# A four-layer graph network on one core: the engines' hand-over in the dense stage, the source rows of the first edge layer, and the mask's type

## The reference, cut to what matters

```python
# layer 0
edge_input = concat(h[src], edge_attr_32)
messages = gelu(edge_input @ mW1 + mb1) @ mW2 + mb2
gates = sigmoid(gelu(edge_input @ gW1 + gb1) @ gW2 + gb2)
aggregated = segment_sum(messages * gates, dst)
update = gelu(concat(h, aggregated) @ uW1 + ub1) @ uW2 + ub2
x = x + layernorm(h + update) * ln_g + ln_b
# layer 1
e = (relu(concat(h[src], h[dst]) @ Wm1 + bm1) @ Wm2 + bm2) * edge_attr_96
x = x + relu(concat(h, segment_sum(e, dst)) @ Wu1 + bu1) @ Wu2 + bu2
# layer 2: segment_sum(h[src] @ W + b, dst) / max(deg, 1)
# layer 3: three graph convolutions, norm_src and norm_dst around segment_sum
```

## Time and profile before

| what | us |
|---|---|
| median of 3 runs (6865.93 to 6893.16) | 6881.36 |
| the profiled execution's own time | 6877.96 |
| its span, first to last instruction | 6876.1 |
| PE busy, share of the span | 4438.8, 65% |
| DVE busy | 3951.5, 57% |
| ACT busy | 3522.4, 51% |
| POOL busy | 4259.0, 62% |

### The profile page before, as it was taken

How to read it: one execution, slowest core, us unless ns; L and a number is a source line. 1 busy time by engine, 2 the same in 40 slices (tenths; PEclk the granted TensorE clock), 3 DMA queues, 4 the chain that set the end, 5 groups by cost and what they waited for, 6 DMA issues and landing times. The chain is left out here.

```text
span 6876.1 us, 104878 instructions
## 1 busy us (share of the span) xinstructions
PE 4438.8 (65%) x19614; PEld 2908.5 (42%) x19614; DVE 3951.5 (57%) x12722; ACT 3522.4 (51%) x8822; POOL 4259.0 (62%) x4323
## 2 busy tenths in 40 slices
PE   5768888888886777776887776554555555322222
PEld 2225566555663333333444443444444444222222
DVE  5667777777775666665555554666666344322222
ACT  6987887888885776775555553222222222111110
POOL 0005454555546777775777776775775776677777
PEclk9998988999887888887888887555555555555555
DMA  0003333333332333332444444665554899433332
GB/s 16 0 5 85 102 102 97 102 102 102 102 98 73 77 78 75 76 75 68 118 119 116 119 118 103 161 160 141 123 129 120 119 126 127 79 76 78 79 84 66
DMA packets 958039, 652.70 MB, mean 95 GB/s; under 512 B 730453, under 2 KB 834785, under 8 KB 957946
## 3 DMA queue, kind: packets, MB, share of 16 engines
q1 hardware_dynamic: 819962, 483.05, 25.0%
q0 software_dynamic: 137984, 168.67, 16.2%
HBM read 420.24 MB, written 232.62 MB: 95 GB/s over the span
## 5 line engine op out<-in xcount | busy, mean ns | idle before, releaser
L610 POOL DMA_INDIRECT got<-info_d,idx x784 | 776.8, 991 | 1258.6 <-issue 732.5
L610 POOL DMA_INDIRECT xs<-t,idx x1176 | 1110.8, 945 | 502.4 <-issue 347.7
L1031 PE MATMUL bank<-w,aggT 96*128 96x96 f32 (+1 forms) x3136 | 773.9, 428 | 470.5 <-DVE aggT L1293 470.4
L1024 PE MATMUL bank<-ident,msg 128*96 128x128 f32 (+1 forms) x1568 | 424.3, 426 | 991.3 <-ACT msg L848 819.7
L1031 PEld LDWEIGHTS bank<-w,aggT 96*128 96x128 f32 (+1 forms) x3136 | 703.5, 329 | 581.8 <-issue 500.7
L610 POOL DMA_INDIRECT xs<-c,idx x784 | 748.3, 954 | 314.9 <-issue 233.1
L848 ACT ACTIVATE msg<-xs,now 128x96 f32<-128x96 f32 x784 | 229.3, 363 | 1297.3 <-DMA xs<-c,idx 679.3
L1024 PEld LDWEIGHTS bank<-ident,msg 128*96 128x96 f32 (+1 forms) x1568 | 290.1, 218 | 1052.0 <-ACT msg L848 678.8
L1293 DVE TENSOR_TENSOR_SCAN aggT<-goes,aggT,bank 96x512 f32<-96x512 f32 (+1 forms) x490 | 621.2, 1268 | 135.0 <-DMA goes<-goes_d 63.1
L701 ACT ACTIVATE hd<-xd,nmr,rstd 128x96 f32<-128x96 f32 x1568 | 599.1, 454 | 27.0 <-DVE nmr L1182 27.0
L610 POOL DMA_INDIRECT xs<-in_x_dram,idx x392 | 473.3, 1207 | 173.9 <-issue 119.2
(11 more groups left out here) (189 smaller groups left out, 10722.2 us busy)
## 6 DMA issues: line engine op xcount, KB each, us to landing
goes<-goes_d SPq DMA_DIRECT2D x392, 256.0 KB
t<-xo SPq DMA_DIRECT2D x392, 192.0 KB, 3.5
t<-xn SPq DMA_DIRECT2D x294, 192.0 KB, 2.3
xd<-in_x_dram SPq DMA_DIRECT2D x196, 192.0 KB, 2.4
out_dram<-oo SPq DMA_DIRECT2D x196, 192.0 KB
goes<-goes_d SPq DMA_DIRECT2D x196, 192.0 KB
xd<-t SPq DMA_DIRECT2D x196, 192.0 KB, 4.0
c<-xn SPq DMA_DIRECT2D x196, 192.0 KB, 3.7
```

What stands on the lines that cost most here:

```text
L610: nc.gpsimd.indirect_dma_start(out=into, out_offset=None, in_=table, in_offset=bass.IndirectOffsetOnAxis(ap=indices, axis=0)).then_inc(don ...
L1024: ins = nc.tensor.transpose(bank[g.at(2)][0:m, c * P:(c + 1) * P], msg[:, g.at(2), c, 0:m], ident[:])
L1031: ins = nc.tensor.matmul(tok(bank[2 + g.at(2)], m)[:, c, :], aggT[0:m, g.at(3), c * P:(c + 1) * P], w2[:] if k == 0 else w3[:, k - 1, :], ...
```

## The change

Four edits. (1) In the dense stage the functions of PE and ACT get lags that are one larger from `evac1` and `evac2` on (`evac1` 0 to 1, `z1` 0 to 1, `gelu1` 1 to 2, `out1` 1 to 2, and likewise for layer 1's; `norm_y` 2 to 3), and the order within a step changes on ACT, PE and DVE. The lags of `plus_x` and `finish_x` stay. (2) In the dense stage POOL also gathers x[src], two indirect DMAs of 128 rows a round into `xs`, and SP stores them to a new DRAM table `x_src` in the order of the edges (`x_src_store`, lag 5, ahead of `info_keep`). (3) In e0 POOL gathers only x[dst]; SP loads the source rows from `x_src` (`xs_load`, one plain DMA a round). (4) The mask `goes` and its DRAM copy are float16; a start-up scratch buffer that lay in it moves to `hd`.

```diff
@@ -130,8 +130,9 @@
         dstp = dram("dstp", (E_PAD + 2,), I32)
-        goes_d = dram("goes_d", (E_PAD,))
+        goes_d = dram("goes_d", (E_PAD,), F16)
         info_d = dram("info_d", (HI * LO, 2))
+        x_src = dram("x_src", (E_PAD, D))
         t1 = dram("t1", (E_PAD + N, D))
@@ -165,7 +166,7 @@
         st_p = sb("st_p", [P, ET], I32)
-        st_goes = sb("st_goes", [P, ET])
+        st_goes = sb("st_goes", [P, ET], F16)
         edge_pad = sb("edge_pad", [1, 2], I32)
@@ -214,8 +215,7 @@
         msg = sb("msg", [P, 2, G, D + 1])
-        goes = sb("goes", [P, 3, GE])
-        iota_lo_i = goes[:, 0:2, :].rearrange("p s e -> p (s e)")[:, 0:LO].bitcast(I32)
+        goes = sb("goes", [P, 3, GE], F16)
         tanh_g = sb("tanh_g", [D, 2, GE])
@@ -228,6 +228,7 @@
         degi, cum = (xn[0:HI, :, :, :].rearrange("p s c d -> p (s c d)")[:, i * LO:(i + 1) * LO] for i in range(2))
+        iota_lo_i = hd[:].rearrange("p s c d -> p (s c d)")[:, 1024:1024 + LO].bitcast(I32)
         has, home = (b[0:HI, :, :, :].rearrange("p s c d -> p (s c d)")[:, 0:LO] for b in (xo, oo))
@@ -298,13 +299,13 @@
                    dict(x_in=(6, 1, 1), x1_out=(6, 1, 1), x2_out=(3, 1, 1), o_out=(3, 1, 1), idx_in=(2, 1, GT),
-                        got=(2, 2 * GI * GT, GT), kept=(2, 1, GT)))
+                        got=(2, 2 * GI * GT, GT), kept=(2, 1, GT), xs=(6, GI, 1), c_out=(6, 1, 1)))
         dn["root"] = Count(sem("root_dn"))
...
                             tok_g=1, tok=1, gate=1, msg=1, agg=1, z=1, g=1, u=1, y=1, my=1, norm_y=1, yx=1, xb=1, xr=1),
-                   edge_slots)
+                   {name: edge_slots[name] for name in edge_slots if name != "xs"} | dict(x_in=(6, 1, 1)))
         more("attr", (EG - 1) % 3, 16)
@@ -421,6 +422,10 @@
                     sp.sem_inc(sp_turn, 1)
+                    for i in range(GT):
+                        was = g.shift(i)
+                        need(sp, dn["xs"][was.at(6)], freed(was, 6, GI))
+                        sp.sem_inc(sp_turn, 1)
                     idx_columns(dn, g, NG, GI, slice(0, 2))
@@ -458,15 +463,22 @@
-            pipelined(sp, NG, [(info_idx, 0), (dense_load, 1), (info_keep, 6), (dense_store_x1, 8), (dense_store_x2, 11)])
+            def x_src_store(g):
+                need(sp, dn["xs"][g.at(6)], landed(g, 6, GI))
+                sp.sem_inc(sp_turn, 1)
+                sp.dma_start(x_src[bass.ds(g.j * GI * P, GI * P), :].rearrange("(c p) d -> p c d", p=P),
+                             xs[:, g.at(6), 0:GI, :]).then_inc(dn["c_out"][g.at(6)].sem, 16)
+
+            pipelined(sp, NG, [(info_idx, 0), (dense_load, 1), (x_src_store, 5), (info_keep, 6), (dense_store_x1, 8), (dense_store_x2, 11)])
...
                             was = g.shift(i)
-                            need(sp, ph["xs"][was.at(6)], freed(was, 6, G))
-                            sp.sem_inc(sp_turn, 1)
+                            if "xs" in ph:
+                                need(sp, ph["xs"][was.at(6)], freed(was, 6, G))
+                                sp.sem_inc(sp_turn, 1)
                             if "xd" in ph:
@@ -509,10 +521,17 @@
-                pipelined(sp, EG, [(gather_idx(ph, planes), 0), (edge_load, 3), (goes_load, 5), (edge_store, done)])
+                def xs_load(g):
+                    need(sp, ph["norm_s"], g.j - 5)
+                    sp.sem_inc(sp_turn, 1)
+                    sp.dma_start(xs[:, g.at(6), :, :], edge_view(x_src, g.j * GE)).then_inc(ph["x_in"][g.at(6)].sem, 16)
+
+                pipelined(sp, EG, [(gather_idx(ph, planes), 0)] + ([(xs_load, 1)] if ph is e0 else []) + [(edge_load, 3), (goes_load, 5), (edge_store, done)])
             sp.wait_ge(goes_out, 16)
-            edge_phase(e0, t1, slice(0, 2), 11)
+            for s in range(6):
+                need(sp, dn["c_out"][s], ended(NG, 6, s))
+            edge_phase(e0, t1, slice(1, 2), 11)
             for s in range(3):
@@ -625,6 +644,10 @@
                                dn["got"][half(g)])
+                need(pool, dn["c_out"][g.at(6)], freed(g, 6))
+                pool.sem_inc(pool_turn, 1)
+                for c in range(GI):
+                    gather(xs[:, g.at(6), c, :], a["x"][:, :], idx[:, half(g), 0, col + c:col + c + 1], dn["xs"][g.at(6)])
@@ -645,10 +668,11 @@
                     pool.sem_inc(pool_turn, 1)
+                    for c in range(G if ph is e1 else 0):
+                        gather(xs[:, g.at(6), c, :], t[:, :], idx[:, half(g), 0, col + c:col + c + 1], ph["xs"][g.at(6)])
+                    which = 1 if ph is e1 else 0
                     for c in range(G):
-                        gather(xs[:, g.at(6), c, :], t[:, :], idx[:, half(g), 0, col + c:col + c + 1], ph["xs"][g.at(6)])
-                    for c in range(G):
-                        gather(xd[:, g.at(6), c, :], t[:, :], idx[:, half(g), 1, col + c:col + c + 1], ph["xd"][g.at(6)])
+                        gather(xd[:, g.at(6), c, :], t[:, :], idx[:, half(g), which, col + c:col + c + 1], ph["xd"][g.at(6)])
@@ -738,7 +762,7 @@
             def norm_y(g):
-                standard(dn, g, tok(bank[2 + 4 * g.at(2)]), 2, 1)
+                standard(dn, g, tok(bank[2 + 4 * g.at(2)]), 3, 1)
@@ -764,7 +788,7 @@
             act.wait_ge(weights_in, 16 * n_weights[0])
-            pipelined(act, NG, [(gelu1, 1), (relu2, 5), (norm1, 0), (norm2, 4), (norm_y, 2), (evac1, 0), (evac2, 4)])
+            pipelined(act, NG, [(evac1, 1), (evac2, 5), (gelu1, 2), (relu2, 6), (norm_y, 3), (norm1, 0), (norm2, 4)])
@@ -933,7 +957,7 @@
             pe.wait_ge(idx_step, 1)
-            pipelined(pe, NG, [(out1, 1), (out2, 5), (tr1, 0), (tr2, 4), (z1, 0), (z2, 4)])
+            pipelined(pe, NG, [(z1, 1), (z2, 5), (out1, 2), (out2, 6), (tr1, 0), (tr2, 4)])
@@ -1217,7 +1241,7 @@
                 dve.sem_inc(dve_turn, 1)
-                pair_stats(tok(bank[2 + 4 * g.at(2)]), mv[:, g.shift(2).at(3), 1, :, :]).then_inc(dn["my"].sem, 1)
+                pair_stats(tok(bank[2 + 4 * g.at(2)]), mv[:, g.shift(3).at(3), 1, :, :]).then_inc(dn["my"].sem, 1)
@@ -1259,12 +1283,12 @@
             def dense_state(g):
-                return upto(g, NG, (dn["norm"], g.j - 2), (dn["norm_y"], g.j - 4), (dn["norm2"], g.j - 6),
-                            (dn["mx"], g.j + 1), (dn["my"], g.j - 1), (dn["mz"], g.j - 3))
+                return upto(g, NG, (dn["norm"], g.j - 2), (dn["norm_y"], g.j - 5), (dn["norm2"], g.j - 6),
+                            (dn["mx"], g.j + 1), (dn["my"], g.j - 2), (dn["mz"], g.j - 3))
             dve.wait_ge(info_out, 16)
-            pipelined(dve, NG, [(times_g(dn), 4), (finish_x, 7), (plus_x, 4), (finish_o, 7), (plus_b, 4), (mom_x, 0),
-                                (mom_y, 2), (mom_z, 4), (roots_of(dn, dense_state), 0, NG + 4)])
+            pipelined(dve, NG, [(finish_x, 7), (mom_y, 3), (finish_o, 7), (mom_x, 0), (times_g(dn), 4), (plus_x, 4),
+                                (plus_b, 4), (mom_z, 4), (roots_of(dn, dense_state), 0, NG + 4)])
             for s in range(3):
@@ -1299,7 +1323,10 @@
                 def edge_moments(g):
-                    need(dve, ph["xs"][g.at(6)], landed(g, 6, G))
+                    if first:
+                        need(dve, ph["x_in"][g.at(6)], landed(g, 6))
+                    else:
+                        need(dve, ph["xs"][g.at(6)], landed(g, 6, G))
                     need(dve, ph["xd"][g.at(6)], landed(g, 6, G))
```

## The result

| | us |
|---|---|
| predicted | 6628 (6535 to 6765) |
| after, median of 4 runs | 7260.53 (7255.95 to 7270.57) |
| before, median of 4 runs on the same chip | 6881.18 (6865.93 to 6893.16) |
| ratio, 95% interval | 1.0555 (1.0531 to 1.0578) |

A forecast was written before the change was run, and what follows sets the result against it. It took POOL's gathers to bound the first edge stage and the other engines' hand-over the dense stage, where POOL would take over. Gains of 31, 207 and 15 us made 253 off 6877.96: 6628 as median, range 6535 to 6765.

The forecast's parts named there:

- Dense stage, the hand-over: Dense stage: with the new lags a loop through PE and ACT takes 7.13 us a round, 0.3 under 7.44.
- the loss to the clock: Dense stage: 0.42 us a round of today's loss carried over, so PE, ACT and DVE could do 7.55 us.
- POOL's 7.80: Dense stage: with six gathers a round POOL becomes the bound at 7.80 us a round, ends 7.50 and 8.18.
- The draining behind it: End of the dense stage: POOL ends at 2045 us and e0 starts at 2063, 31 us earlier than before.
- The new waits and the extra DMA on SP: Dense stage: the new waits on POOL and SP and one more plain DMA a round on SP cost nothing.
- e0: First edge stage: without the x[src] gathers the round falls from 11.21 to 9.1 us, gain 207 us, ends 275 and 109.
- The mask: Conv k = 2: 16-bit mask halves its bytes, scan time unchanged, gain 15 us from a range of 0 to 47.
- The lock: Dense stage: DVE's two-SBUF-input work blocks POOL, 9.70 us a round, 372 us more, 7000 in all; chance 0.04.
- e0's exchange taking the gap: First edge stage: PE's and ACT's waits grow, round 10.1 us, gain 109 instead of 207, total 6726; chance 0.17.
- That x_src brings nothing: First edge stage: bound by DVE's chain of roots at 11.2 us, only 46 us left, total 6835; chance 0.03.
- The one with the sign right: Dense stage: the slower rival, POOL blocked by DVE's two-SBUF-input work, 7000 us in all; chance 0.04.
- the same sum: Whole kernel: gains of 31, 207 and 15 us, 253 off 6877.96, giving 6625, or 6628 for the median.

The follow-up runs named there:

- dve_order: The changed kernel with DVE's dense step reordered, finish_x and finish_o at lag 8 and the moments last before the roots: 6953.97 us, ratio 1.0110.
- nogap: dve_order with out1, out2 first on PE, and on ACT gelu1, relu2 ahead of the evacuations and norm_y ahead of norm1: 6555.03 us, ratio 0.9511.
- finish8: The changed kernel with only the lag of finish_x and finish_o raised from 7 to 8: 7209.96 us, ratio 1.0462.
- full_order: nogap with DVE's dense step reordered, finish_x behind mom_x instead of after times_g: 6530.57 us, ratio 0.9477.
- act_order: dve_order with gelu1 and relu2 ahead of the evacuations on ACT and norm_y last: 7113.03 us, ratio 1.0341.
- lags_only: The kernel before with only edit (1), the dense stage's new lags and orders on PE, ACT and DVE: 7589.33 us, ratio 1.1034.
- gather_only: The changed kernel with edit (1) undone, edits 2 to 4 kept: 6550.23 us, ratio 0.9519.

## Why the dense stage lost its clock

How the low clock and the gap hang together is read from one stretch at 0.50 each of before, after, dve_order and nogap, in this order (columns as in the earlier trace rows):

```profile
1444.40:1454.40 10.00, 10.00 (x36) 7.42 (x35) 5.57 (x20) 6.29 (x16) 3.78 (x4) 0.50 0.28 81
```

```profile
938.00:1010.00 72.00, 63.83 (x220) 47.29 (x220) 35.26 (x128) 39.92 (x98) 34.85 (x36) 0.50 0.29 83
```

```profile
1058.00:1208.00 150.00, 133.85 (x466) 100.28 (x465) 78.70 (x287) 82.07 (x205) 82.27 (x84) 0.50 0.31 89
```

```profile
1280.30:1290.40 10.10, 10.09 (x36) 7.65 (x36) 7.70 (x32) 7.28 (x18) 7.76 (x8) 0.50 0.70 215
```

In before, a round at low clock is 36 matmuls in 10.0 us, and PE does not wait at all: its own instructions have grown longer and cover ACT's. It is granted the full clock again after 10.2 us, in each of the 33 such stretches of that dense stage (mean clock 0.87; the stage's start and end, where PE has little to do, are left out here and below). In after, 220 matmuls are 6.1 rounds: 11.8 us each, PE busy 10.4 of them and waiting 1.35 for gelu1. This wait is 1.35 us at either clock, since evac2 and gelu1 start when PE has finished and PE starts when they have. Here 38 of the 40 low stretches last 24 to 120 us (in dve_order they last 14 to 150, in finish8 68 to 140 but for three of 3.4), and at full clock the round is 7.59 us, at low clock 11.8 (13.3 where the clock changes within it). The mean of 11.52 is mostly the time at low clock. nogap has the 10.0 us back, in most of its low rounds without a wait, and its full clock comes back after 10.2 us in 61 of 63 stretches, after 6.8 in the other two.

The full clock is also lost sooner in after. It holds for 10.2 us at a time, in 40 of 41 stretches; in before for 7 to 96 us, 35 on average. One such stretch of after as a window, and two of its rows of PE:

```profile
1009.70:1019.90 10.20, 5.68 (x36) 4.07 (x35) 8.58 (x29) 6.33 (x17) 3.46 (x3) 1.00 0.31 89
```

```profile
1011.25 1.07 PE L912 MATMUL bank<-hdT,uw 96*96 96x512 f32 x2 [1.35 <-ACT u L775]
...
1018.21 0.65 PE L919 MATMUL bank<-ident,hd 128*96 128x128 f32 x4 [2.38 <-ACT hd L725]
```

PE is busy for 5.7 of these 10.2 us: beside the 1.35 for gelu1 it waits 2.38 us for norm1 (`hd`), which on ACT stands behind norm_y, and norm_y waited 3.66 us for the roots there. In the full-clock stretches of before PE is busy for 75 to 81%.

Two things speak against the length of a wait as the whole cause. In 18 of nogap's 61 stretches of 10.2 us PE did stand still, for up to 0.61 us, and the clock came back all the same; in full_order it did so after waits of up to 0.79 us. And in act_order the clock stayed low through stretches in which no wait of PE was longer than 0.49 us, eight of its 27, of 65 to 120 us. The longest:

```profile
690.60:810.10 119.50, 115.35 (x396) 85.65 (x396) 64.92 (x243) 69.82 (x177) 64.41 (x67) 0.50 0.32 92
```

What is shown: edit (1)'s orders and lags make the loss (lags_only, gather_only); the low round of 11.8 us is PE's 10.4 and the wait of 1.35, with the ring closed or open (after, finish8); the time is lost in long stretches at 1.2 instead of 2.4 GHz; and two moves of order, with the lags kept, bring the stage back (nogap). Every order with the wait of 1.35 us in each round has low stretches of 120 us and more. That this wait is what keeps the clock low is argued and not shown: act_order stays low without it, and nogap changes ACT's and PE's order at once, so that which of the two the clock answers to was not separated. What the chip counts was not measured, and is not guessed.

## Why the prediction was wrong, by its own steps

**The step that failed** is in "Dense stage, the hand-over": "With today's loss to the clock (7.86 - 7.44 = 0.42) PE, ACT and DVE could do a round in 7.55 us." The loop itself was found, but a round wholly at full clock took 7.59 us and not 7.13, more than the 7.33 of before: the ring below held it (with the ring open, in finish8, three such rounds took 6.9 to 7.4). The larger part is the clock. The same loop holds all of PE's step and a stretch in which PE must stand still. At half the clock PE's part of it is 10.4 us and the standing still is added, 11.8; and the loss to the clock, taken over as 0.42, was the price in a kernel whose PE had no such gap. The loss became 11.52 - 7.59 = 3.9 us a round. The numbers for it stood in the text: the earlier trace rows showed the clock at 0.77 beside 1.00, and nothing was asked about what ends a low stretch.

**A ring not seen**: out2 to finish_x, roots, norms, tr2 and back in two rounds. By itself it costs little (finish8, 50 us), though with DVE's whole order turned 318 us came back (dve_order), which stays unexplained beyond the 50.

**POOL's 7.80** was right where nothing hid it: 7.80 in full_order, 7.99 in gather_only, 7.97 in nogap. The draining behind it was taken too short: in full_order POOL's last gather started at 2045 us, as forecast, but e0 at 2078 and not 2063. So even this version gains 15 us before e0 where 31 were forecast, and gather_only loses 25. In after POOL was not the bound. The new waits and the extra DMA on SP cost nothing that can be seen: gather_only and full_order have them all.

**e0** was right in mechanism and too small in size. ACT's wait for the roots, 189.5 us, is no longer among the waits; one single wait of 20.7 us for roots is left, on another line, at the start of the stage. The other terms were held too high: 9.1 us a round forecast, 8.00 measured; gain 318 instead of 207, outside its ends (109 to 275). The two waits for hid, 0.48 and 0.34 us, and 0.5 for tr were added to ACT's 7.88. Measured, those for hid come to 0.5 and 1.5 us over the whole stage, the wait for tr to 24.8 (0.27 a round), and ACT's own work is 755 / 98 = 7.70; 7.70 + 0.27 = 7.97 is the round. PE's work for the same matmuls fell from 8.75 to 7.31 us a round, with the clock at 0.98 instead of 0.85. PE was seen as kept "busier" and granted "more clock"; the drop of 1.44 us that this makes was not carried through.

**The mask** was right, 15 us forecast and 15 measured; that the figure is met so exactly is luck, since 15 was picked from a range of 0 to 47. Its scan and the DMA of k = 2 (5715 to 6240 us, packets, MB, share), after:

```profile
L1317 DVE TENSOR_TENSOR_SCAN aggT<-goes,aggT,bank 96x512 f32<-96x512 f16 x392 | 497.2, 1268 | 111.1 <-DMA goes<-goes_d 47.2 <-PE bank L1015 29.7 <-PE bank L1048 25.4
...
L1317 DVE TENSOR_TENSOR_SCAN aggT<-goes,aggT,msgT 96x512 f32<-96x512 f16 x98 | 124.9, 1274 | 0.5 <-DVE msgT L1340 0.5
```

```profile
q1 hardware_dynamic: 81688, 33.22, 24.3%
...
goes<-goes_d SPq DMA_DIRECT2D x100, 128.0 KB, 5.5
```

1.268 and 1.274 us with a 16-bit operand against 1.269 and 1.274: the width changes nothing in DVE's time here. The queue holds 24.3% instead of 32.1, with 33.22 MB instead of 46.04, and DVE's wait for the mask in that stage fell from 63.1 to 47.2 us.

**The rivals.** The lock did not come (mean gathers of 0.94 to 1.00 us in the dense stage of every kernel). The e0 row that spoke for it is weaker than it was read: that gather had started 0.25 us before the first of the DVE operations, and these ran on for 0.55, 1.27 and 0.53 us, no longer than elsewhere, so only POOL was held up. e0's exchange taking the gap (0.17) did not either: the opposite. That x_src brings nothing (0.03): no. The slower case that came was not among them. The one with the sign right was priced on POOL's side, while edit (1), the only one that touches PE, was given a gain with no way to lose. With that edit left out the same sum would have had 6550 in its range, though partly by luck: e0's extra gain of more than 110 us covers the 56 us by which the dense stage fell short (25 lost where 31 were to be gained).

## What to carry to other kernels

When engines pass work to and fro, look for a stretch in which the matrix engine waits for something that starts only when it stops; price this loop once for each clock level seen in the trace, since another engine's work that PE's own covers is covered still better when PE slows, and a gap stays as long as it was (1.35 us at either clock). Put an instruction of another group between the producer and the consumer on both engines (here out1, out2 first on PE, gelu1 first on ACT; the two moves were only run together). Larger lags did not do this here: the change and nogap have the same ones on PE and ACT, and the order within the step made the difference. An order that ends one engine with what the other begins with makes a ring (act_order).

## What the runs showed of the hardware that was not expected

- The granted clock came back to 1.00 after 10.2 us in all 33 stretches of before in which PE worked through at 0.50, and in 61 of nogap's 63, some with waits of up to 0.61 us. It stayed at 0.50 mostly for 24 to 120 us in after, where PE stood still 1.35 us a round, but for up to 120 us in act_order too, with no wait over 0.49. In the middle of e0, with a round of 8.00 instead of 11.20 us, it stood at 1.00 where before had 0.86.
- Taking the gathers of x[src] away from e0 also made those of x[dst] cheaper, 0.987 to 0.956 us, and the source gathers themselves went from 1.207 us in e0 to 0.944 in the dense stage of after (0.973 in gather_only), though DVE's two-operand work stands beside them there as well.
- On two chips of the set the engines paused in every turn of the loops, in every kernel: before takes 9081 or 9192 us there instead of 6881, and a gain of 4.8% (gather_only) reads as a loss of 0.7%. A ratio from such a chip is no measure of the change.
